# Sigmoid attention on one core: one fixed order of score, value and other steps in every cycle

## What is computed

```python
q = (query @ Wq.T).reshape(B, L, H, D) * scale
k = (key @ Wk.T).reshape(B, -1, H, D)
v = (value @ Wv.T).reshape(B, -1, H, D)
scores = jax.nn.sigmoid(jnp.einsum('blhd,bshd->bhls', q, k))
o = jnp.einsum('bhls,bshd->blhd', scores, v).reshape(B, L, E)
return o @ Wo.T
```

## Time and profile before

| | |
|---|---|
| median of three runs | 2683.96 us |
| the profiled execution, its span | 2685.0 us |
| TensorE (PE) busy | 2547.9 us, 95% |
| VectorE (DVE) busy | 1627.2 us, 61% |
| ScalarE (ACT) busy | 1572.9 us, 59% |
| GpSimd (POOL) busy | 322.9 us, 12% |
| chain that ended last, by engine | PE 82%, DVE 8%, ACT 4% |
| the sigmoid attention's cycles, first score step to last value group | 1281 to 1749 us of the span |

### The profile page before, as it was taken

How to read it: one execution, slowest core, us unless ns; L and a number is a source line. 1 busy time by engine, 2 the same in 40 slices (tenths; PEclk the granted TensorE clock), 3 DMA queues, 4 the chain that set the end, 5 groups by cost and what they waited for, 6 DMA issues and landing times.

```text
span 2685.0 us, 46470 instructions
## 1 busy us (share of the span) xinstructions
PE 2547.9 (95%) x18464; PEld 1263.7 (47%) x18464; DVE 1627.2 (61%) x2991; ACT 1572.9 (59%) x2691; POOL 322.9 (12%) x278
## 2 busy tenths in 40 slices
PE   7999999999899899999899999989989999999987
PEld 3334344343477777775233333268733343434433
DVE  6878888879376764441112221057587788878854
ACT  1787777777601221111687978932237778778773
POOL 2010100100013302210011010012211001010001
PEclk8999999999999999999999999999979999999997
DMA  5433334322300010001754546110043343234300
GB/s 123 74 37 39 62 45 67 45 31 26 94 10 16 1 55 16 1 1 53 110 61 74 71 65 74 49 52 1 13 62 62 44 68 45 32 62 51 37 1 32
DMA packets 68636, 125.13 MB, mean 47 GB/s; under 512 B 20979, under 2 KB 45630, under 8 KB 64966
## 3 DMA queue, kind: packets, MB, share of 16 engines
q1 hardware_dynamic: 67270, 119.73, 29.1%
q10 hardware_dynamic: 1152, 2.44, 0.4%
HBM read 41.59 MB, written 2.10 MB: 16 GB/s over the span
## 4 chain that ended last, share of the span: by engine, by line
PE 82%; DVE 8%; ACT 4%; issue 2%; SPq 2%; DMA 1%; ACTq 0%; POOL 0%; POOLq 0%; DVEq 0%
PE psum L203 39%; PE psum L749 20%; PE psum L214 13%; PE psum L2118 7%; DVE mpart L939 4%; ACT probs L817 3%; PE psum L309 1%; SPq L1061 1%; PE psum L2111 1%; PE psum L759 0%; DVE x L1406 0%; PE psum L768 0%; DMA qst<-qp_lo 0%; SPq L1062 0%; ACT kp_hi L806 0%
## 5 line engine op out<-in xcount | busy, mean ns | idle before, releaser
L817 ACT ACTIVATE probs<-psum 128x512 f32<-128x512 f32 (+3 forms) x2080 | 1266.1, 690 | 270.5 <-PE psum L203 262.4
L939 DVE TENSOR_REDUCE mpart<-psum 128x2 f32<-128x804 f32 x1024 | 971.0, 990 | 223.6 <-PE psum L203 211.1
L749 PE MATMUL psum<-probs,vt 128*17 128x512 f32 (+1 forms) x4992 | 653.2, 602 | 3.6 <-ACT probs L817 2.9
L203 PE MATMUL psum<-qst,kst 64*128 64x512 f32 (+3 forms) x2496 | 608.7, 440 | 18.3 <-ACT probs L817 7.7
L203 PE MATMUL psum<-kst,qst 62*128 62x402 f32 x2048 | 469.3, 410 | 29.1 <-DVE mpart L939 26.2
L203 PEld LDWEIGHTS psum<-qst,kst 64*128 64x128 f32 (+3 forms) x2496 | 284.3, 182 | 386.3 <-issue 199.9
L203 PEld LDWEIGHTS psum<-kst,qst 62*128 62x128 f32 x2048 | 227.2, 191 | 304.1 <-DVE mpart L939 189.9
L749 PEld LDWEIGHTS psum<-probs,vt 128*17 128x17 f32 (+1 forms) x4992 | 92.5, 96 | 212.8 <-issue 177.0
L214 PE MATMUL psum<-wv,ctxT 128*32 128x256 f32 (+1 forms) x2448 | 171.0, 398 | 0.3 <-DVE kp_lo L920 0.3
L214 PE MATMUL psum<-ctxT,wk 128*32 128x512 f32 (+1 forms) x1536 | 146.6, 507 | 10.6 <-DMA ctxT<-in_ctxT 9.2
L2163 ACT ACTIVATE inner<-psum 128x512 f32<-128x512 f32 x32 | 19.1, 597 | 214.6 <-PE psum L2118 214.6
(11 more groups left out here) (337 smaller groups left out, 2626.4 us busy)
## 6 DMA issues: line engine op xcount, KB each, us to landing
kst<-kp_hi SPq DMA_DIRECT2D x144, 200.1 KB, 5.9
ctxT<-in_ctxT SPq DMA_DIRECT2D x36, 512.0 KB, 5.3
kst<-kp_lo SPq DMA_DIRECT2D x72, 200.1 KB, 5.4
qst<-qp_hi SPq DMA_DIRECT2D x144, 64.0 KB, 4.6
kst<-kp_hi SPq DMA_DIRECT2D x84, 100.1 KB, 2.9
qst<-qp_lo SPq DMA_DIRECT2D x72, 64.0 KB, 5.1
kst<-kp_lo SPq DMA_DIRECT2D x42, 100.1 KB, 3.0
stage<-in_L_ffn_W SPq DMA_DIRECT2D x16, 256.0 KB, 4.3
```

Source lines behind the costliest of these rows:

```text
L203: last = e.matmul(dst, lhsT, rhs, start=i == 0, stop=i == len(pairs) - 1)
L749: t = e.matmul(c.bank(self.acc)[32 * h:32 * h + VW, :], self.vt[0:kn, kc, self.head(g, h), :], p[0:kn, h % self.wide, :], start=kc == 0, s ...
L817: e.activation(self.probs[n % slots][0:kn, :, :], c.psum[0:kn, k:k + self.wide, :], ACT.Exp if softmax else ACT.Sigmoid, scale=DH ** -0.5) ...
L939: e.tensor_reduce(self.mpart[:, :, p * (SEQ // P) + qt, i], c.psum[:, k:k + 2, 0:MAX_WIDTH], AX.X, ALU.max).then_inc(c.drained(k), 1)
```

## The change

The table of the sigmoid attention becomes one string for all cycles and all groups.

```diff
 ORDERS = (
-    (
-        ("sssvfvs", "sfvsssv", "fssvvss", "svfssvs", "sfvsssv", "fsssvfvs", "ssvv"),
...
-        ("ssvvss", "vssvss", "fssvvss", "sfvfsssv", "fssvvss", "svfssvfs", "ssfvv"),
-    ),
+    (("ssvvffffss",) * 7,) * GROUPS,
     (
```

More of the change, by code:

```diff
@@ L53 @@
 ORDERS = (
-    (
-        ("sssvfvs", "sfvsssv", "fssvvss", "svfssvs", "sfvsssv", "fsssvfvs", "ssvv"),
-        ("ssfvfssv", "sfvsssvf", "ssvvss", "sfvsssv", "fssvvss", "sfvsssv", "fssvv"),
-        ("fsssvfsv", "sfvsfssv", "fsssvvs", "sfsssvfv", "sfssvvs", "svssvs", "svsv"),
-        ("ssvvss", "vssvss", "fssvvss", "sfvfsssv", "fssvvss", "svfssvfs", "ssfvv"),
-    ),
+    (("ssvvffffss",) * 7,) * GROUPS,
     (
```

## The result

The changed kernel takes 2762.58 us (median of 4 runs, 2760.42 to 2766.18) against 2684.1 us for the kernel before on the same chip (2681.84 to 2686.22). The ratio is 1.0296, with a 95% interval of 1.0279 to 1.0314: slower by 3.0%. The prediction was 2751 us, with 2730 to 2782 as its range.

The account below looks back on a forecast made before the run. The prediction took TensorE's program order as the bound, with slack in ScalarE. Its terms, -16.1 + 89.3 + 19.2 - 25.5 = +66.9 us on 2683.96, gave 2751 us, range 2730 to 2782.

Parts of the forecast that it names:

- main case: Whole kernel: the summed forecast of 2751 us, with its own range 2736 to 2766 and a chance of 0.76.
- Part 1: Sigmoid attention on TensorE: 52 fewer stretches of score steps at 0.31 us each, -16.1 us.
- Part 2: Stretches of four score steps: the fourth waits for the first's sigmoid, 0.96 us lost in each of 93, +89.3 us.
- Part 3: Pairs of projections or a transpose back to back on bank 7 wait for the copy between them, +19.2 us.
- Part 4: Old TensorE waits in the sigmoid attention, for DMA and sigmoids, shrink from 33.0 to 7.5 us, -25.5 us.
- The switches decide: Rival: the fourth score step's wait is mostly filled and fewer stretches make it faster, 2668 us with that alone; chance 0.05.
- ScalarE sets the pace: Rival: only ScalarE's 416 sigmoids at 0.91 us count, order hardly does, 2684 us; chance 0.06.
- The clock rival: Rival: TensorE's pauses lower its clock in about every fourth of 112 cycles, some 34 us more, 2785 us; chance 0.13.

Follow-up runs that it names:

- kernel with two and two: Changed kernel with each cycle reordered to two score steps, one value group, the same again, then the other work: 2711.19 us, 1.0104 of the kernel before.

## Why the prediction was right, and where it was off

**What bounds the kernel.** Right. TensorE's program order set the time, and ScalarE had slack in it: the same instructions took 79 us more by their order. The median of 2762.6 us lies within the main case's own range, 2736 to 2766, near its upper end. That range was made for errors in the latencies and in parts 3 and 4. More than half of the 12 us that were missing came from the clock instead, for which the main case had nothing, so the time alone is kinder to the prediction than its terms are.

**Part 1, fewer stretches.** The prices of 0.23 and 0.20 us hold in every kernel here (0.66 for two, 0.89 for three, in each). The changed kernel has the 118 stretches that I counted, 93 of them of four. The kernel with two and two has 89 more and is still 51 us faster, so the switches never decided.

**Part 2, the fourth step.** The mechanism is the one found, shown from two sides: with stretches of at most three the wait is next to gone, and with one pair of banks less it is back at short stretches. Its size was a little low: the sigmoid starts 0.61 us behind the first step, not 0.57, so the value group starts 2.11 us after the first step where I had 2.08, and the mean over the stretches of four is 2.13, low clock included. 0.05 more in each of 93 makes 4.8 us.

**Part 3, other work back to back.** 3.31 us for the key pairs (3.34), 2.46 for output projections (2.47); a value projection's pair takes 1.66 us from start to start, so it costs 0.79 instead of 0.74. 19.2 us was right within 1, and splitting half of the pairs gave back the 9.7 us that it should.

**Part 4, the waits of before.** Right in the main: unit 1 takes 32.3 us, 32.2 by my prices without any wait, and its second query projection starts without one. The run with the context later shows that most of the old wait and the low clock behind it were worth some 5 us in the profile. What I had not seen is that the low clock at the start would last twice as long, 6.8 us: by my prices the start costs some 5 us instead of the 4 that I took, and the 1 us that I left for the query did not come.

**The clock.** This is the term that was missing from the sum: I had it as a rival (every fourth cycle, 34 us) and as nothing in the main case. It fell five times behind the start, and each time the two value groups took 1.1 to 1.5 us longer, some 7 us in all. The reason that I gave against the clock, that a pause here is under 1 us, was not so by my own part 3: its wait of 1.4 us stands right ahead of part 2's of 0.7 in six cycles, and I had summed them apart. All five falls are in these six cycles, but the runs do not show that the two waits together are what brings a fall: the first pair had none, and the kernel with the old table in group 2 has falls with no key projection near. With 4.8 us of part 2 that is the 12 us by which the sigmoid attention (547.3 us against 535) and the median (2762.6 against 2751) exceed the forecast.

**The rivals.** "The switches decide" fell: the fourth step's wait is there in every cycle. "ScalarE sets the pace" fell too: ScalarE's idle time ahead of sigmoids, 70.3 us before, is 144.9 now. The clock rival came about in part, with 5 falls where it had 28. Its price was not summed rightly: a fall in every fourth of 112 cycles is 28 x 1.36 = 38 us, not 34, which would have been 2789 us.

## What to carry to other kernels

Take two engines that hand each other work through a ring of n buffers, where the consumer has caught up at the start of each round. If the producer's uninterrupted stretch is longer than n, step n + 1 can't start before the consumer has started and finished the first one. Here that was 1.68 us after the first step, and 0.96 us or a little more was lost in each round. Then the consumer in turn has nothing to do while the producer does its other work (1.05 us here). So write the order in stretches of at most n, and put the other work between them. The runs show this for three pairs of banks and for two. To price a new order, take the costs from start to start in the trace of the old one, count stretches, and then follow one round by hand; do it with two waits side by side wherever two terms of the sum fall into the same cycle.

## What was not expected of the hardware

TensorE's clock fell where it had waited twice within a few microseconds, for 1.41 and 0.71 us, but not every time, and elsewhere behind waits of 0.2 and 0.4 us. It stayed at 2.4 GHz through dozens of cycles in a row with one wait of 0.7 us each (granted clock 1.00 from 1670 to 1830 us in the changed kernel). The same stretch of code, unit 14 in the old order, had a low clock in the kernel before and none in the kernel with the context later: 25.9 us and 24.2. And a load can be late because of what stands ahead of it in the queue that issues it: four issues took SyncE 4.16 us.
